# Reordering a recurrent-attention kernel on one core: the order of products on TensorE, of four early steps, and a last output in three pieces

## What is computed

```python
xn = layernorm(x)
q, k, v = (silu(xn @ W) for W in (Wq, Wk, Wv))      # 16 heads of 16
o = lightning_attn(q, k, v, log_decay, chunk=128)   # scores inside a chunk, a decayed state between chunks
o = o * sigmoid((xn @ Wg1) @ Wg2)
o = o * rsqrt(mean over each head of o*o + eps) * norm_w
g = silu(dequantised(fp8(xn * scale)) @ dequantised(fp8(W2 * scale1)))
out = x + (o @ Wo) * g
```

## Time and profile before

| what | value |
|---|---|
| median of 3 runs | 128.74 us (128.6 to 129.91) |
| the profiled execution's own time | 128.68 us |
| its span in the trace | 126.9 us |
| time around the span | 1.78 us |
| busy: PE, DVE, ACT, POOL | 114.7, 101.7, 81.4, 80.8 us |

### The profile page before, as it was taken

The page is one execution under the profiler, slowest core; times in us unless marked ns, Lnnn a source line. Parts: engine busy times, 40 slices in busy tenths (PEclk is TensorE's granted clock), DMA queues, the critical chain, the costliest instruction groups (busy, mean ns, idle before and its releaser), DMA issues.

```text
span 126.9 us, 6394 instructions
## 1 busy us (share of the span) xinstructions
PE 114.7 (90%) x2688; PEld 99.3 (78%) x2688; DVE 101.7 (80%) x271; ACT 81.4 (64%) x156; POOL 80.8 (64%) x119
## 2 busy tenths in 40 slices
PE   3979989988999999999999999999999999867680
PEld 3979889758978898879978898889788987556560
DVE  1899999989895899869994999498939891497781
ACT  7689989969967656684677378558673664811100
POOL 6716599899839683968677884968384839100070
PEclk9999999999999999999999999999999999999997
DMA  2769800020000400033003300150006040000015
GB/s 84 235 175 339 273 3 3 5 45 6 5 0 10 83 0 5 5 62 108 3 5 65 111 0 5 41 132 5 0 20 150 5 126 5 5 5 5 0 67 181
DMA packets 11067, 7.57 MB, mean 60 GB/s; under 512 B 4832, under 2 KB 11040, under 8 KB 11040
## 3 DMA queue, kind: packets, MB, share of 16 engines
q1 hardware_dynamic: 11040, 7.17, 20.2%
HBM read 3.50 MB, written 2.10 MB: 44 GB/s over the span
## 4 chain that ended last, share of the span: by engine, by line
POOL 31%; issue 29%; DVE 20%; ACT 9%; PE 6%; DMA 2%; POOLq 0%; DVEq 0%
POOL e_q L408 5%; POOL e_sum L403 5%; POOL y L441 5%; POOL kd L419 4%; DVE probs L764 4%; POOL rstd L396 3%; POOL own_mid L423 2%; POOL qd L413 2%; DMA x_sb<-in_L_attn_x_dram 2%; POOL on_lo L446 1%; PE b_s L1307 1%; DVE bn L729 1%; POOL own_end L423 1%; DVE og L797 1%; DVE xqT L754 1%
## 5 line engine op out<-in xcount | busy, mean ns | idle before, releaser
L1092 PE MATMUL b_kv<-w_hi,xT_hi 128*128 128x256 f32 x64 | 16.8, 284 | 0.0
L1093 PE MATMUL b_kv<-w_lo,xT_hi 128*128 128x256 f32 x64 | 16.5, 281 | 0.0
L441 POOL TENSOR_TENSOR y<-sg,x_sb 128x512 f32<-128x512 f32 x7 | 9.0, 1286 | 10.4 <-DVE sg L902 10.3
L446 POOL TENSOR_TENSOR on_lo<-on,on_hi 128x512 fp32r<-128x512 f32 x6 | 7.7, 1278 | 12.3 <-ACT on_hi L620 12.3
L403 POOL TENSOR_TENSOR e_sum<-e_y,e_magic 128x512 f32<-128x512 f32 x8 | 10.3, 1285 | 7.2 <-DVE e_magic L748 7.2
L797 DVE SCALAR_TENSOR_TENSOR og<-gate_tanh,b_o 128x512 f32<-128x512 f32 x7 | 4.8, 687 | 11.8 <-PE b_o L1243 11.8
L1095 PE MATMUL b_kv<-w_hi,xT_lo 128*128 128x256 f32 x64 | 12.7, 280 | 0.0
L1243 PE MATMUL b_o<-probs,v_par 64*32 64x64 f32 x896 | 12.6, 222 | 0.0
L413 POOL TENSOR_TENSOR qd<-q_silu,q_decay 128x512 f32<-128x512 f32 x8 | 10.3, 1293 | 3.3 <-ACT q_silu L550 3.3
L1092 PEld LDWEIGHTS b_kv<-w_hi,xT_hi 128*128 128x128 f32 x64 | 12.0, 188 | 0.2 <-issue 0.2
L1093 PEld LDWEIGHTS b_kv<-w_lo,xT_hi 128*128 128x128 f32 x64 | 12.1, 188 | 0.0
(11 more groups left out here) (205 smaller groups left out, 366.6 us busy)
## 6 DMA issues: line engine op xcount, KB each, us to landing
out_dram<-y SPq DMA_DIRECT2D x7, 256.0 KB, 2.5
x_sb<-in_L_attn_x_dram SPq DMA_DIRECT2D x4, 384.0 KB, 5.4
own_cross<-own_end SPq DMA_DIRECT2D x12, 64.0 KB, 2.0
qd_cross<-qd SPq DMA_DIRECT2D x12, 64.0 KB, 2.4
x_sb<-in_L_attn_x_dram SPq DMA_DIRECT2D x2, 256.0 KB, 3.5
w_f<-in_L_attn_Wq_dram SPq DMA_DIRECT2D x1, 256.0 KB, 3.8
w_f<-in_L_attn_Wk_dram SPq DMA_DIRECT2D x1, 256.0 KB, 4.0
w_f<-in_L_attn_Wv_dram SPq DMA_DIRECT2D x1, 256.0 KB, 4.5
```

The lines of the kernel that those rows point to most:

```text
L441: g.tensor_tensor(y[:, n % 2], sg[:, n % 2].rearrange("p (s d) -> p s d", s=S), x_sb[:, x_tiles(n), :], ALU.add).then_inc(s_y, 1)
L446: g.tensor_tensor(on_lo[:], on[:, n % 2], on_hi[:].bitcast(F32), ALU.subtract).then_inc(s_onlo, 1)
L1092: t.matmul(dst[:, s], xT_hi[:, u, kk, tok], w_hi[:, w, kk], start=(s == 0 and kk == 0), stop=False, skip_group_check=True)
L1093: t.matmul(dst[:, s], xT_hi[:, u, kk, tok], w_lo[:, w, kk], start=False, stop=False, skip_group_check=True)
```

## The change

Nothing is computed differently; the order of some instructions is, and the last output leaves in three pieces.

- In PE's loop, from_chunk(n, 0, 0) moves ahead of gate(n+1), so that the gate's product stands next to the transposes of x; ffn(n+1) moves behind from_chunk(n, 1, 1), so that it stands next to the second half of the output projection (of step 6, which has none, next to state_steps(7)).
- ACT, start: silu_v(0) ahead of silu_q(0); find_over(1) ahead of gate(1); square_o(0) ahead of scale_y(2).
- DVE, start: gate_o(0) ahead of low_xT(2). DVE, end: gate_o(7) ahead of root_pair_last(6).
- The end: the second sequence's 256 columns are projected, multiplied, added and stored in two pieces of 128 columns, in a list LAST of three pieces in place of two.

```diff
+        LAST = [(0, slice(0, D), b_s[:, 0:D], b_kv[:, 0:D]),
+                (1, slice(0, D // 2), b_s[:, 512:512 + D // 2], b_kv[:, 512:512 + D // 2]),
+                (1, slice(D // 2, D), b_o[:, 512:512 + D // 2], b_kv[:, 512 + D // 2:512 + D])]
...
-            for s in range(S):
-                sp.wait_ge(s_lasty, s + 1)
-                sp.dma_start(out_v[:, last.start + NB * s, :], y[:, 2, s]).then_inc(s_laststored, 16)
+            for m in range(len(LAST)):
+                s, cols, ps, prod = LAST[m]
+                sp.wait_ge(s_lasty, m + 1)
+                sp.dma_start(out_v[:, last.start + NB * s, cols], y[:, 2, s, cols]).then_inc(s_laststored, 16)
...
-            silu_q(0)
             act.wait_ge(s_vzero, 2)
             silu_v(0)
+            silu_q(0)
...
+            find_over(1)
             gate(1)
-            find_over(1)
             high_xT(2)
             act.wait_ge(s_dvec, 4)
             silu_ffn(1)
+            square_o(0)
             scale_y(2)
-            square_o(0)
             silu_ffn(0)
...
+            def product_last(m):
                 n = STEPS - 1
+                s, cols, ps, prod = LAST[m]
+                dve.wait_ge(s_outps, n * S + m + 1)
                 dve.wait_ge(s_ffn, n + 1)
+                v.tensor_tensor(prod, ps, ffn_silu[:, n % 3, s * D + cols.start:s * D + cols.stop], ALU.mult).then_inc(s_lastsg, 1)
+
+            def add_x_last(m):
                 n = STEPS - 1
+                s, cols, ps, prod = LAST[m]
+                dve.wait_ge(s_lastsg, m + 1)
+                v.tensor_tensor(y[:, 2, s, cols], prod, x_sb[:, x_tiles(n).start + NB * s, cols], ALU.add).then_inc(s_lasty, 1)
...
             stats(3)
+            gate_o(0)
             low_xT(2)
-            gate_o(0)
...
             root_last(n - 1)
+            gate_o(n)
             root_pair_last(n - 1)
-            gate_o(n)
             head_norm(n - 1)
...
+            def project_o_last(m):
+                n = STEPS - 1
+                s, cols, ps, prod = LAST[m]
+                pe.wait_ge(s_onlast, s + 1)
+                for kk in range(KH):
+                    mm = t.matmul(ps, on[:, n % 2, kk, s * P:s * P + P], wo_scaled[:, kk, cols], start=(kk == 0),
                                   stop=(kk == KH - 1), skip_group_check=True)
                 mm.then_inc(s_outps, 1)
...
                 state_steps(n)
+                from_chunk(n, 0, 0)
                 gate(n + 1)
-                from_chunk(n, 0, 0)
                 if known(n + 2):
                     transpose_x(n + 2)
...
                 from_state(n)
+                from_chunk(n, 1, 1)
                 ffn(n + 1)
-                from_chunk(n, 1, 1)
...
-            for s in range(S):
-                project_o(n, s)
+            for m in range(len(LAST)):
+                project_o_last(m)
```

More of the change, by code:

```diff
@@ L191, in layer_kernel @@
         ps_sum_last = b_s[:, 0:C]
-        ps_prod_last = [b_kv[:, 0:D], b_kv[:, 512:512 + D]]
-        ps_last = [b_s[:, 0:D], b_s[:, 512:512 + D]]
+        LAST = [(0, slice(0, D), b_s[:, 0:D], b_kv[:, 0:D]),
+                (1, slice(0, D // 2), b_s[:, 512:512 + D // 2], b_kv[:, 512:512 + D // 2]),
+                (1, slice(D // 2, D), b_o[:, 512:512 + D // 2], b_kv[:, 512 + D // 2:512 + D])]
         s_x = [sem(f"x_loaded_{n}") for n in range(4)]
@@ L375, in _ @@
             last = x_tiles(STEPS - 1)
-            for s in range(S):
-                sp.wait_ge(s_lasty, s + 1)
-                sp.dma_start(out_v[:, last.start + NB * s, :], y[:, 2, s]).then_inc(s_laststored, 16)
+            for m in range(len(LAST)):
+                s, cols, ps, prod = LAST[m]
+                sp.wait_ge(s_lasty, m + 1)
+                sp.dma_start(out_v[:, last.start + NB * s, cols], y[:, 2, s, cols]).then_inc(s_laststored, 16)
             sp.wait_ge(s_stored[0], 16 * (STEPS // 2))
             sp.wait_ge(s_stored[1], 16 * (STEPS // 2 - 1))
-            sp.wait_ge(s_laststored, 16 * S)
+            sp.wait_ge(s_laststored, 16 * len(LAST))
         @block.gpsimd
@@ L884, in head_norm_last @@
                                 ps_rs.rearrange("p k (s c t) -> p s k c t", s=S, c=2)[:, s], ALU.mult).then_inc(s_onlast, 1)
-            def product_last(s):
+            def product_last(m):
                 n = STEPS - 1
-                dve.wait_ge(s_outps, n * S + s + 1)
+                s, cols, ps, prod = LAST[m]
+                dve.wait_ge(s_outps, n * S + m + 1)
                 dve.wait_ge(s_ffn, n + 1)
-                cols = slice(s * D, s * D + D)
-                v.tensor_tensor(ps_prod_last[s], ps_last[s], ffn_silu[:, n % 3, cols], ALU.mult).then_inc(s_lastsg, 1)
-            def add_x_last(s):
+                v.tensor_tensor(prod, ps, ffn_silu[:, n % 3, s * D + cols.start:s * D + cols.stop], ALU.mult).then_inc(s_lastsg, 1)
+            def add_x_last(m):
                 n = STEPS - 1
-                dve.wait_ge(s_lastsg, s + 1)
-                v.tensor_tensor(y[:, 2, s], ps_prod_last[s], x_sb[:, x_tiles(n).start + NB * s, :], ALU.add).then_inc(s_lasty, 1)
+                s, cols, ps, prod = LAST[m]
+                dve.wait_ge(s_lastsg, m + 1)
+                v.tensor_tensor(y[:, 2, s, cols], prod, x_sb[:, x_tiles(n).start + NB * s, cols], ALU.add).then_inc(s_lasty, 1)
             def product(n):
@@ L1045, in _ @@
             product(n - 1)
-            for s in range(S):
-                product_last(s)
-                add_x_last(s)
+            for m in range(len(LAST)):
+                product_last(m)
+                add_x_last(m)
         @block.tensor
@@ L1279, in project_o @@
             def project_o(n, s):
-                if n == STEPS - 1:
-                    pe.wait_ge(s_onlast, s + 1)
-                elif s == 0:
+                if s == 0:
                     pe.wait_ge(s_on, n + 1)
@@ L1290, in project_o @@
                         pe.wait_ge(s_probs, 4 * STEPS)
-                dst = ps_out[:, s] if n < STEPS - 2 else ps_out_last2[:, s] if n < STEPS - 1 else ps_last[s]
+                dst = ps_out[:, s] if n < STEPS - 2 else ps_out_last2[:, s]
                 if n < STEPS - 2:
@@ L1306, in project_o @@
                 for kk in range(KH):
-                    mm = t.matmul(dst, on[:, n % 2, kk, s * P:s * P + P], wo_scaled[:, kk], start=(kk == 0 and (s == 0 or n == STEPS - 1)),
+                    mm = t.matmul(dst, on[:, n % 2, kk, s * P:s * P + P], wo_scaled[:, kk], start=(kk == 0 and s == 0),
+                                  stop=(kk == KH - 1), skip_group_check=True)
+                mm.then_inc(s_outps, 1)
+            def project_o_last(m):
[4 more added lines that the diff above has]
+                    mm = t.matmul(ps, on[:, n % 2, kk, s * P:s * P + P], wo_scaled[:, kk, cols], start=(kk == 0),
                                   stop=(kk == KH - 1), skip_group_check=True)
```

## The result

The changed kernel takes **130.87 us** (median of 4 runs, 130.7 to 131.21) beside 129.17 us for the kernel before on the same chip (4 runs, 128.6 to 129.91): 1.0152 times as long, 95% interval 1.0097 to 1.0207. I had said 129.0, no change; it is slower by about 2.0 us (1.3 to 2.7). The profiled execution took 130.70 us with a span of 129.0, against 128.68 and 126.9.

The account below looks back on a forecast made before the run. PE's list and the way from_chunk, gate_o, scores were taken as nearly equal bounds. -1.20 + 0.2 + 0.96 + 0.4 = +0.36 on 128.68 gives 129.04, said as 129.0; range 127.8 to 130.0.

Parts of the forecast that it names:

- Parts 1 and 2: PE's loop, both reorderings together: scores 0.24 us earlier per body, taken five times, -1.20 us.
- Part 4: Tail, gate_o(7) ahead of root_pair_last(6): the pair and spread_rs(6) come later and hold head_sums(7), +0.96 us, bounds 0.8 to 1.1.
- Part 5: The end, last output in three pieces: a third store issue costs 0.5 us, a little comes back, +0.4 us in all.
- Part 1: Loop bodies 1 to 5, gate beside x's transposes: the transposes end 0.15 us earlier, and everything behind them too.
- everything behind moves up by 0.15: Loop, step behind the transposes of x: all later work comes 0.15 us sooner, checked only at line 1303, cover 0.09.
- second rival: Loop: bodies gain PE's full share, 0.48 us each, -2.4, so 127.8; mode changes saved are the gain; chance 0.17.
- Part 2: Loop, FFN's product behind the last quarter: gate_o 0.69 us earlier, but scores then wait for silu_ffn, 0.24 per body.
- first rival: Loop: silu_ffn eats the whole gain, with line 1303's thin cover for on_lo, so 130.2 us; no gain in bodies 0.17.
- Part 3: Start, ACT swaps and gate_o(0) ahead of low_xT(2): masks of step 1 later by 0.4, +0.2 us, bounds -0.3 to +0.7.
- all quarters of step 7 end at 114.96: Tail, step: the last quarters' end, 113.28 + 1.68, from which gate_o(7) and the pair were timed in the new order.
- may come back: The end: the last piece is 64 KB, not 128 KB, so a little of the third issue's +0.5 returns, leaving +0.4.
- the ring: Loop body: the way from from_chunk's last quarter through gate_o to the next scores, nearly as long as PE's own list.

Follow-up runs that it names:

- the version with the late projection: Both loop reorderings, project_o(n-1, 0) moved behind the FFN's product, and POOL and ACT moves, against the kernel before: 128.39 against 129.5 us, ratio 0.9933.

## Why the prediction was wrong, point by point

Four things add up to the miss. Parts 1 and 2 gave 0.84 less than their sum had, Part 4 cost 0.56 more and Part 5 0.18 less, and the sum started from 128.68, where the runs beside the changed kernel have 129.17. None of them alone makes up the miss.

**Parts 1 and 2** were summed to -1.20; measured alone -0.36. In Part 1 the step "everything behind moves up by 0.15" failed: I checked line 1303's cover and not transpose_k's, which waits for state_end with no cover at all (0.15 from one to the other in both kernels). The gate alone gained nothing. My sentence in the second rival, that the shorter transposes beside the gate agree with the Trainium skill's rule (TensorEngine Tiling (Array Packing), section Key Properties: a change of tiling mode drains TensorE), was true of those transposes and false of the time, since one change of mode less per body bought nothing. In Part 2 the mechanism was as written: gate_o 0.63 sooner (0.69 said), silu_ffn last before scores. The size was off: of the 0.24 per body 0.15 was Part 1's, and scores follow silu_ffn by 0.22 and not by 0.15, so 0.02 is left; like for like the bodies of n = 2 and 5 gained 0.02 to 0.14, and nothing in the changed kernel's own profile. The first rival had this place right, a body gaining next to nothing, but for another reason: not on_lo late but state_end.

**Part 3** (+0.2) measured +0.2 (0 to 0.4). The chain is there, 0.52 at the masks where I had 0.4; that the whole comes out at the very 0.2 says no more than its interval does.

**Part 4** (+0.96, bounds 0.8 to 1.1) is the term that went beyond its own bounds: 1.5 alone (1.0 to 2.0). Its mechanism is shown by turning PE's order, and its length behind the quarters' end is right, 0.87 and 0.88. What failed is the step "all quarters of step 7 end at 114.96": I took that end from one profile as fixed, in whichever order. Before, head_sums(7) hung on the pair, which is ready whenever the quarters end; now it hangs on the quarters, and these hold a stop of PE that the earlier trace rows hardly show, since it was 0.15 us in that execution. In ten of the other eleven profiles it was 0.31 to 0.99. Behind such a stop the old order gives 1.44 to 1.67 from the quarters' end to head_sums(7) and the new one 2.84, so the swap costs 1.2 to 1.4, and not the 0.88 of a profile with a short stop. That the runs without a profile have the same stops is not shown, only that the 1.5 fits. The changed kernel's own profile is the one without a stop (0.05). There the spans differ by 2.08 us otherwise: the quarters begin 1.13 later (114.41, before 113.28) and take 0.10 less, head_sums(7) is 0.88 further behind them, and the rest to the end is 0.17 longer. Of the 1.13, 0.56 stands at 8 us, ahead of every edit, where PE starts the first projection at 8.77 and not at 8.21, and is scatter.

**Part 5** (+0.4, bounds 0.2 to 0.55) measured +0.2 (-0.2 to 0.6). The third issue costs its 0.48 (0.96 to 1.44), but the last piece lands sooner than I had: 1.67 us from its issue to the end of SP's wait (126.87 to 128.53) against 1.99 for the 128 KB one before (124.47 to 126.46). In all profiles it is 1.66 to 1.68 for 64 KB (three) and 1.99 to 2.00 for 128 KB (nine). The step that failed is what "may come back": 0.32 and not 0.1, which leaves 0.16.

With the measured terms the sum is -0.36 + 0.19 + 1.52 + 0.22 = +1.57, beside 1.96 (1.25 to 2.67) for the whole.

## What to carry to other kernels

Before an instruction is put ahead of others, ask what the old order covered: work that fits into another engine's wait is free only as long as it stands inside that wait, and it covers that wait's scatter too, which one profile doesn't show. When PE's work moves up, go through every wait behind it, not only the one that looks thinnest; a constant distance to another engine's instruction in two profiles names the one that holds. And take out of the ring what nobody in it waits for (here half an output projection), rather than change the order of what all do.

## What the runs showed that I had not expected

PE stops at fixed places of its own list. Counting all of PE's records in order (weight loads, products, semaphore instructions), the stops named here lie at numbers 2241 (scores(3) of the changed kernel, 0.40 us), 3009 (head_sums near 70 us, 0.29 us before, 0.46 to 0.75 in six others and 0.13 to 0.15 in five), 4801 (0.93 us, in the version with the late projection) and 5313 (the last quarters, up to 0.99 us): all 193 past a multiple of 256. With 8 more instructions in the list, number 5313 was still the place, and the work there was 8 instructions earlier in the kernel. Neighbouring products in the quarters mostly start 0.006 to 0.03 us apart. Not every such number has a stop; those seen here fall where many tiny products run close together. The profile also lists a DMA queue for instructions; its row on the page is the same in all twelve profiles but for its share:

```profile
q8 instruction: 21, 0.34, 1.1%
```

0.34 MB in 21 packets are 16 KB each. The Trainium skill (Perfetto Trace Analysis, section The 4-stage abstract model) has instructions of 64 bytes; 256 of them are 16 KB, and 21 times 256 is 5376, beside 5503 records of PE in the kernel before. So the stop is likely PE waiting for the next such packet, which fits the shift by 8. The traces time the packets too, and bear it out. With k counting the packets, each of the 21 stops of 0.28 us and more at the four numbers (256 k + 193, k = 8, 11, 18 and 20) ends 1.21 to 1.50 us behind the end of packet k, and at none of the twenty such numbers of any of the twelve profiles does PE go on sooner than that. Before and in the version with three pieces PE starts the 83rd product of the quarters at the same time (114.12 and 114.11); packet 20 ends at 112.76 and 113.50, and PE goes on at 114.27 and 114.97. That the stop's length follows the packet's end is thus shown by timing; no run here delayed or hastened a packet, so that the packet is its cause stays an inference.
